# Second attention of a two-layer graph network: neighbour sums with one head per matmul, one copy out, and full-height transposes

## The reference

```
xp    = (x @ W).reshape(n, 4, 64)                      # 4 heads of 64
a_src = einsum('nhc,hc->nh', xp, att_src)
a_dst = einsum('nhc,hc->nh', xp, att_dst)
alpha = leaky_relu(a_src[src] + a_dst[dst], 0.2)       # edges and self loops
ex    = exp(alpha - segment_max(alpha, dst)[dst])
w     = ex / segment_sum(ex, dst)[dst]
agg   = segment_sum(xp[src] * w[..., None], dst)
out   = elu(agg.reshape(n, 256) + bias)
x     = layernorm(x + out)
```

## Time and profile before

| | |
|---|---|
| median of 3 runs | 4586.03 us (4585.14 to 4588.12) |
| the profiled execution | 4583.4 us, its span 4581.9 us |
| mean granted TensorE clock | 0.882 of full speed |
| PE, DVE, ACT, POOL busy in the span | 81%, 74%, 61%, 68% |
| first and last gather of the second attention | at 2487.94 us and 4522.89 us of the span |

### The profile page before, as it was taken

How to read it: one execution, slowest core, us unless ns; L and a number is a source line. 1 busy time by engine, 2 the same in 40 slices (tenths; PEclk the granted TensorE clock), 3 DMA queues, 4 the chain that set the end, 5 groups by cost and what they waited for, 6 DMA issues and landing times. The chain is left out here.

```text
span 4581.9 us, 149697 instructions
## 1 busy us (share of the span) xinstructions
PE 3730.9 (81%) x42462; PEld 2550.6 (56%) x42462; DVE 3401.2 (74%) x11603; ACT 2779.6 (61%) x7985; POOL 3137.5 (68%) x3229
## 2 busy tenths in 40 slices
PE   6987988888888888888886877877777888778774
PEld 4654555555555555555554655555555555556553
DVE  3225788777887778877775677788877888877787
ACT  2324555555555555555553777777777777777775
POOL 1227777777777777777772777777777777777773
PEclk9998999999999999999997678777777777876876
DMA  6878998999999999898983777777777777777774
GB/s 204 281 246 238 267 267 263 264 264 264 265 263 265 263 265 266 262 265 263 265 266 100 193 206 210 204 204 206 204 207 208 204 206 206 204 207 209 204 207 129
DMA packets 820557, 1052.06 MB, mean 230 GB/s; under 512 B 458633, under 2 KB 632338, under 8 KB 820464
## 3 DMA queue, kind: packets, MB, share of 16 engines
q0 software_dynamic: 225072, 726.83, 54.0%
q1 hardware_dynamic: 594078, 323.35, 27.4%
q10 hardware_dynamic: 1314, 0.99, 0.1%
HBM read 915.79 MB, written 133.39 MB: 229 GB/s over the span
## 5 line engine op out<-in xcount | busy, mean ns | idle before, releaser
L1286 POOL DMA_INDIRECT plain_rows<-xp,plain_index x1563 | 1559.9, 998 | 555.3 <-issue 438.8
L765 POOL DMA_INDIRECT typed_rows<-kv,typed_index x1563 | 1505.2, 963 | 586.1 <-issue 444.4
L1391 PE MATMUL plain_p_o<-plain_rows,plain_weight_t 128*64 128x130 f32 (+1 forms) x8336 | 855.1, 348 | 43.3 <-DVE plain_weight_t L1417 42.5
L1158 ACT ACTIVATE typed_weight<-typed_weight,typed_col 128x416 f32<-128x416 f32 x521 | 334.7, 642 | 860.5 <-DVE typed_col L990 811.4
L1378 PE MATMUL plain_p_s<-all_cst,plain_rows 128*128 128x128 f32 (+1 forms) x2084 | 453.2, 316 | 360.0 <-DMA plain_rows<-xp,plain_index 358.1
L1391 PEld LDWEIGHTS plain_p_o<-plain_rows,plain_weight_t 128*64 128x64 f32 (+1 forms) x8336 | 569.5, 168 | 202.2 <-issue 128.7
L874 PE MATMUL typed_p_s<-typed_kt,typed_q 64*32 64x416 f32 x4168 | 471.6, 519 | 251.8 <-issue 223.4
L1378 PEld LDWEIGHTS plain_p_s<-all_cst,plain_rows 128*128 128x128 f32 (+1 forms) x2084 | 334.4, 173 | 513.2 <-issue 495.6
L988 DVE CUSTOM_DVE_ANT_0 typed_weight<-typed_p_s,typed_far 128x416 f32<-128x416 f32 x521 | 305.5, 586 | 339.5 <-PE typed_p_s L874 313.4
L1424 DVE CUSTOM_DVE_ANT_0 plain_alpha<-plain_alpha,plain_far 128x416 f32<-128x416 f32 x521 | 309.8, 595 | 309.6 <-ACT plain_alpha L1540 296.9
L961 DVE TENSOR_TENSOR typed_kt<-typed_p_kt,typed_rel 128x768 f32<-128x768 f32 x521 | 494.2, 949 | 4.0 <-PE typed_p_kt L851 3.8
(11 more groups left out here) (191 smaller groups left out, 6299.7 us busy)
## 6 DMA issues: line engine op xcount, KB each, us to landing
typed_match<-match SPq DMA_DIRECT2D x131, 208.0 KB
plain_match<-match SPq DMA_DIRECT2D x131, 208.0 KB
agg<-qkv_zero SPq DMA_DIRECT2D x98, 264.0 KB
typed_agg<-agg SPq DMA_DIRECT2D x98, 264.0 KB
plain_agg<-agg SPq DMA_DIRECT2D x98, 264.0 KB
kv<-qkv_kv SPq DMA_DIRECT2D x98, 258.0 KB
typed_kinds<-match SPq DMA_DIRECT2D x131, 192.0 KB
typed_rows<-kv,typed_index POOLq DMA_INDIRECT x1563
```

Of the source, the lines that this page charges most:

```text
L765: pool.indirect_dma_start(rows[:, r, j, :], None, k.kv, bass.IndirectOffsetOnAxis(ap=index[:, g, at:at + 1], axis=0)).then_inc(rows_in[r], 16)
L1158: act.activation(weight[:, c], weight[:, c], ACT.Exp, bias=col[:, t.slot(4), LOW:LOW + 1]).then_inc(exp_done, 1)
L1286: pool.indirect_dma_start(rows[:, r, j, :], None, k.xp, bass.IndirectOffsetOnAxis(ap=index[:, g, at:at + 1], axis=0)).then_inc(rows_in[r], 16)
L1391: last = pe.matmul(p_o[at:at + HC, t.slot(2), 0:2 * V], weight_t[0:e, t.slot(2), j * P + at:j * P + at + HC], val[:, 2 * V * g:2 * V * g + ...
```

## The change

In `aggregate` each chunk gets four matmuls of 32 weight columns by 65 row columns, one for each head, at the column groups 0, 32, 64 and 96, in place of two of 64 by 130. All four heads' sums then lie in the same 65 columns of `p_o`, and `put` takes them in one 128 x 65 copy. The lent chunk is transposed and multiplied over all 128 rows of the next tile's first chunk, not over 32; the turned weights of the rows past 32 are the zeros that `p_w` was set to.

```diff
             def score(t):
...
                 for j in range(CH + 1):
-                    e = P if j < CH else SPILL
...
-                    a_src = rows[0:e, r, j] if j < CH else rows[0:e, t.back(-1).slot(R), 0]
-                    last = pe.transpose(p_s[:, c, j * P:j * P + e], a_src[:, A_SRC:A_DST],
-                                        ident[0:e, 0:e])
+                    a_src = rows[:, r, j] if j < CH else rows[:, t.back(-1).slot(R), 0]
+                    last = pe.transpose(p_s[:, c, j * P:j * P + P], a_src[:, A_SRC:A_DST], ident)
                 last.then_inc(scores_ready, 1)
...
             def aggregate(t):
...
                 for j in range(CH + 1):
-                    e = P if j < CH else SPILL
-                    val = rows[0:e, t.slot(R), j] if j < CH else rows[0:e, t.back(-1).slot(R), 0]
-                    for g in range(2):
-                        at = HC * g
-                        last = pe.matmul(p_o[at:at + HC, t.slot(2), 0:2 * V], weight_t[0:e, t.slot(2), j * P + at:j * P + at + HC],
-                                         val[:, 2 * V * g:2 * V * g + 2 * V],
+                    val = rows[:, t.slot(R), j] if j < CH else rows[:, t.back(-1).slot(R), 0]
+                    for h in range(HEADS):
+                        at = TN * h
+                        last = pe.matmul(p_o[at:at + TN, t.slot(2), 0:V], weight_t[:, t.slot(2), j * P + at:j * P + at + TN],
+                                         val[:, V * h:V * h + V],
                                          start=j == 0, stop=j == CH, tile_position=(0, at), skip_group_check=True)
                 last.then_inc(agg_done, 1)
...
             def put(t):
...
                 act.copy(result[:, m, V:AG], col[:, m, KEEP:KEEP + 1])
-                for h in range(HEADS):
-                    at = TN * h
-                    last = act.copy(result[at:at + TN, m, 0:V], p_o[at:at + TN, t.slot(2), V * (h % 2):V * (h % 2) + V])
-                last.then_inc(result_ready, 1)
+                act.copy(result[:, m, 0:V], p_o[:, t.slot(2), 0:V]).then_inc(result_ready, 1)
```

## The result

The changed kernel takes 4604.86 us (median of six runs, 4600.07 to 4608.88), the kernel before, measured beside it, 4587.39 us (4585.14 to 4590.88): ratio 1.0037, 95% interval 1.0024 to 1.0050. It is slower by 17 us, above the range given (4573 to 4595 us), and on the side that had a chance of 0.09. The profiled execution has a span of 4601.1 us, 19.2 us more than before. Three rows divide that up.

The account below looks back on a forecast made before the run. GpSimd's gathers bound the second attention: 2487.9 us ahead, 2035 of gathers, 59 to the end, 1.5 around. Less 2.0 us at the end, 4583.4 becomes 4581.4, on the runs' footing 4584 us; range 4573 to 4595.

Parts of the forecast that it names:

- the side that had a chance of 0.09: Outcome slower than the kernel before: VectorE's passes in worse places (0.07) or TensorE setting the pace (0.02).
- The frame: Second attention: GpSimd's gathers set the pace, 3.91 us a tile, gaps about 0.30 us; TensorE and ScalarE follow.
- TensorE becomes the pace: Rival, second attention: at 1.2 GHz TensorE needs 4.21 us a tile if sums gain nothing, 4740 us; chance 0.02.
- the gain counts in full: Rival: the sums set the pace, so 0.53 us a tile gives 276 us, 4308 us; chance 0.01.
- The end: Behind the last gather: earlier sums and copies save 2.0 us, between nothing and 3 us.
- The sums: TensorE, second attention: 0.66 to 1.32 us a tile, 350 to 690 us busy instead of 855.1, hidden behind gathers.
- The copies: ScalarE, second attention: four copies become one, busy time from 423.4 us to near 112 us, hidden behind gathers.
- The 62 ns a MATMUL: Rule against the change: TensorE's 32 sums would take 1.98 us a tile; set aside for the measured 0.66 us.
- the gather's length: GpSimd's mean gather, 998 ns with 79.7 us of stretching in all: change taken as zero, within 7 ns.
- They shift into worse places: Rival: VectorE's passes stretch gathers more, slower from 7.2 ns a gather, 4600 us at 10 ns; chance 0.07.
- the stretched gather of 3507.01 us: GpSimd gather of 1.35 us, cited as stretched by VectorE's rectifier pass running from 3507.67 to 3508.25 us.
- The upper bound of 142 us: Most that longer gathers could add, if every tile's VectorE pass cost the largest stretch of 425 ns.

Follow-up runs that it names:

- j1: The changed kernel with one extra ScalarE copy of 128 by 64 ahead of the score's move; 4609.93 us, ratio 1.0060.
- j3: The changed kernel with three extra ScalarE copies of 128 by 64 ahead of the score's move; 4571.89 us, ratio 0.9977.
- g3: The changed kernel with VectorE's rectifier and mask passes each reading one operand from PSUM, not both from SBUF; 4535.25 us, ratio 0.9897.
- k1: The kernel before with VectorE's rectifier and mask passes each reading one operand from PSUM, not both from SBUF; 4546.08 us, ratio 0.9915.
- m1: The kernel before with one copy out in place of four, taking wrong columns for two of the four heads; 4607.91 us, ratio 1.0053.
- a1: The changed kernel with four copies out of 32 by 64 again, new sums and wide transposes kept; 4576.62 us, ratio 0.9984.
- h1: The kernel before with VectorE's rectifier pass issued behind two small column operations instead of ahead of them; 4606.36 us, ratio 1.0045.

## Why the prediction was wrong

**The frame was right.** The second attention is paced by GpSimd; its gaps stayed at 0.3 us; TensorE and ScalarE are followers; the rivals "TensorE becomes the pace" and "the gain counts in full" did not come.

**The sizes were right.** The end shortened by some 2 us (2.0 forecast). The sums went from 855.1 to 460.7 us (350 to 690 forecast); at 1.2 GHz a tile's take 1.10 us, where I took 1.32 between 0.66 and 1.32. The copies went to 108.9 us (112 forecast), ScalarE's busy time fell by 363 us, 2779.6 to 2416.2 on the pages (310 forecast). The 62 ns a MATMUL that the Trainium skill, "TensorE: Matmul & The Clock Gate", section "Wait — 56ns, not 53.3ns?", gives without hardware decoding are not seen here either: 32 records take 0.66 us.

**The step that failed** is the gather's length: "If they hit the sensitive part of a gather as often as now, the term is zero. I take zero". It was +20.1 us (13 ns over 1563 gathers), the rival "They shift into worse places", at 0.07. The argument for zero was that the landings scatter and so the passes fall now early, now late. They do scatter, but not evenly: with one copy out the mask pass starts just ahead of a gather 240 times instead of 164. By chance it would be 168, so the kernel before stood about at an even spread, and a change of the rhythm could go either way; some tenths of a microsecond of ScalarE work changed the sign (j1, j3). A term of 80 us that hangs on relative timing was given 0.17 of the chance for both signs together, when nothing in the profile tied it down. I put the middle of its size at 10 ns, which is about what came; the chance was too small, and the range of 7 ns too narrow.

**A reading that was wrong, too.** The prediction put the stretched gather of 3507.01 us to the rectifier pass of 3507.67 us. The row ahead of it in the same trace is the one that held it; it runs from 3506.96 to 3507.55, and 0.81 us later the gather ends:

```profile
3506.96 0.59 DVE L1424 CUSTOM_DVE_ANT_0 plain_alpha<-plain_alpha,plain_far 128x416 f32<-128x416 f32 x1 [0.22 <-ACT plain_alpha L1540]
```

One could have seen it: the pass that holds a gather must be running when the gather starts. The upper bound of 142 us was too low for the same reason: it let one pass a tile hold a gather, where two passes can.

**Shown and not shown.** Shown: the loss is stretched gathers (the two traces, g3, k1), nearly all held by a pass with two SBUF operands that began first; the part of the change that brought them is the one copy (m1, a1). Not shown: why with less ScalarE work the mask pass starts ahead of gathers more often. ScalarE then waits for scores 283 to 311 times instead of 135 to 178, so its move follows the landing of rows more directly, and landings follow gathers; but inside the changed kernel the 299 tiles with an idle ScalarE (over 0.15 us) ahead of the move hold less stretch than the other 222, 164 and 214 ns a tile, where in the kernel before it was 174 ns in 156 tiles and 120 in 365 (counted in the traces). So the tiles without such a wait became worse too. And h1 has few such waits (123) and 1013 ns. This stays open.

## What to carry to other kernels

Where a GpSimd stream of gathers sets the pace, "hidden behind it" is not the end of the argument: ask which VectorE operations with two SBUF operands run beside it (here such operations held gathers in every case that began in time), and price the stretch (mean less median, times the count) as an unknown of both signs whenever any follower's timing changes. Better, take the conflict away: an operand of each of the two passes in PSUM instead of SBUF took 61 ns off the mean gather here, and 1.4% off the changed kernel (0.9897 against 1.0037). And judge a change to a follower by a version in which that conflict is gone, since there the same change went from 17 us slower to 11 us faster; and split that gain too, of which here only some 3 us lay where the change acts.

## What the hardware showed that I had not expected

- A gather of 128 rows can be held only near its start: 0.13 us in, by an operation that began before it. Held gathers end 0.82 us behind that operation, and took up to 1372 ns in both kernels; a pass begun in a gather's first 0.15 us held none (1044 cases).
- What matters is where the operands lie, not how long the operation is: passes of 0.58 us and block work of 0.42 us with two SBUF operands hold a gather, a pass of 0.65 us with an operand in PSUM and a copy of 0.67 us from PSUM do not. The exception is `plain_res`, with one full tile from SBUF (98 cases).
- The form of 32 by 65 in four column groups costs 1.10 us for 32 records at 1.2 GHz and 0.66 us at 2.4 GHz, 1.7 times and not twice.
- The same reordering of three VectorE operations was worth -26 us on one kernel and +24 us on the other.
